# One kernel of four fused layers: the output projection in fp32r parts, another order in the opening, another form of the last multiply

## The reference

```
x = x + L0(x)  # conv over 16 tokens (taps from cond) -> Wp -> B_t = softplus, C_t = tanh; u = x@Ws
               # state = decay*state + dt*B_t*u_t ;  y = C_t*state (64 wide) ; y @ Wo + bo
x = x + L1(x)  # LSTM: a = x@Wx + b + h@Wh ; i,f,o = sigmoid, g = tanh ; c = f*c + i*g ; h = o*tanh(c)
x = x + L2(x)  # token shift, 16 experts by hashed token id: relu(x@wk)**2 @ wv, times a sigmoid gate
x = x + L3(x)  # threshold t per (sequence, feature): L3(x) = x * (|x| >= t)
```

## Time and profile before

| | us |
|---|---|
| median of three runs | 4284.19 |
| profiled execution, its own time | 4276.5 |
| its span, first to last instruction | 4274.8 |
| TensorE busy, share of the span | 3840.3 (90%) |
| VectorE | 3104.3 (73%) |
| ScalarE | 1775.6 (42%) |
| GpSimd | 618.9 (14%) |

### The profile page before, as it was taken

One profiled execution on the slowest core, in us unless ns is written; L12 is line 12 of the kernel. 1 busy time (PEld: TensorE's weight loads), 2 busy tenths in 40 slices (PEclk: granted clock), 3 DMA queues, 4 the chain that ended last, 5 costly groups with the idle time before them and its releaser, 6 DMA issues. The chain is left out here.

```text
span 4274.8 us, 115998 instructions
## 1 busy us (share of the span) xinstructions
PE 3840.3 (90%) x45058; PEld 2624.1 (61%) x45058; DVE 3104.3 (73%) x9883; ACT 1775.6 (42%) x5459; POOL 618.9 (14%) x657
## 2 busy tenths in 40 slices
PE   3799999999999999999999999999599999989900
PEld 3466666666656666665666666665378878869900
DVE  8777787777777777787777787755454455439989
ACT  2233433333433333433333433333244444338866
POOL 4011110110110110110110111110100000005634
PEclk8899999999999999999999999999899999999955
DMA  5211001111001111010011010000234333415412
GB/s 209 88 31 36 26 29 31 31 32 33 26 29 31 30 31 35 26 33 27 28 32 36 26 33 26 26 19 12 104 118 158 137 118 128 154 59 163 155 71 86
DMA packets 143014, 267.65 MB, mean 63 GB/s; under 512 B 19589, under 2 KB 85637, under 8 KB 139458
## 3 DMA queue, kind: packets, MB, share of 16 engines
q1 hardware_dynamic: 120896, 185.19, 12.9%
q0 software_dynamic: 17696, 66.79, 4.3%
q10 hardware_dynamic: 3938, 8.96, 0.6%
HBM read 177.33 MB, written 83.92 MB: 61 GB/s over the span
## 5 line engine op out<-in xcount | busy, mean ns | idle before, releaser
L424 PE MATMUL bank<-buf,buf 128*16 128x256 f32 x32768 | 1873.3, 380 | 68.5 <-DVE buf L695 56.8
L424 PEld LDWEIGHTS bank<-buf,buf 128*16 128x16 f32 x32768 | 906.3, 97 | 904.7 <-DVE buf L695 101.9
L797 PE MATMUL bank<-buf,buf 128*128 128x256 f32 (+1 forms) x3584 | 1181.7, 330 | 25.2 <-DVE buf L1182 22.4
L798 PE MATMUL bank<-buf,buf 128*128 128x256 f32 (+1 forms) x3584 | 1121.3, 313 | 0.0
L799 PE MATMUL bank<-buf,buf 128*128 128x256 f32 (+1 forms) x3584 | 1120.6, 313 | 0.0
L611 DVE SCALAR_TENSOR_TENSOR buf<-buf,buf,buf 128x256 f32<-128x256 f32 x1920 | 880.4, 485 | 0.8 <-issue 0.8
L673 DVE STREAM_TRANSPOSE buf<-bank 128x256 f32<-128x256 f32 x1024 | 458.7, 448 | 544.5 <-PE bank L424 510.6
L797 PEld LDWEIGHTS bank<-buf,buf 128*128 128x128 f32 x3584 | 677.1, 189 | 275.9 <-issue 237.6
L570 ACT ACTIVATE buf<-buf 128x96 f32<-128x96 f32 x1024 | 290.6, 284 | 1208.4 <-DVE buf L678 1208.0
L799 PEld LDWEIGHTS bank<-buf,buf 128*128 128x128 f32 x3584 | 678.7, 189 | 41.2
L798 PEld LDWEIGHTS bank<-buf,buf 128*128 128x128 f32 x3584 | 679.9, 190 | 38.5
(11 more groups left out here) (132 smaller groups left out, 3035.8 us busy)
## 6 DMA issues: line engine op xcount, KB each, us to landing
buf<-in_wk SPq DMA_DIRECT2D x16, 2048.0 KB, 9.7
buf<-in_wv SPq DMA_DIRECT2D x16, 2048.0 KB, 9.8
buf<-in_xT SPq DMA_DIRECT2D x62, 496.0 KB, 3.9
buf<-x_scratch SPq DMA_DIRECT2D x31, 544.0 KB, 4.3
buf<-in_xT SPq DMA_DIRECT2D x32, 512.0 KB, 3.7
expert_in_scratch<-buf POOLq DMA_DIRECT2D x16, 1024.0 KB, 22.2
x_scratch<-buf SPq DMA_DIRECT2D x32, 512.0 KB, 5.0
buf<-expert_in_scratch SPq DMA_DIRECT2D x16, 1024.0 KB, 11.7
```

The source lines that it names most:

```text
L424: last = mm(gate_ps[hf][32 * j:32 * j + B, 0:HCOLS], hist[:, k, at_step(slot_at)], wh[:, k, j * GCOLS + hf * HCOLS:j * GCOLS + (hf + 1) * ...
L797: nc.tensor.matmul(out, left[0], right[0], start=first, stop=False)
L798: nc.tensor.matmul(out, left[0], right[1], start=False, stop=False)
```

## The change

It does four things.

1. **Output projection by parts.** y and Wo are cut into high and low parts in fp32r. The 64 rows of high y and 64 rows of low y stand above each other (`y_pair`, 128 rows) against high Wo twice (`wo_pair`); a second matmul takes high y again with ones (`y_high`, 97 rows used) against low Wo, high bo and low bo (`wo_rest`). So eight fp32r matmuls of 128 and 97 rows stand where four fp32 matmuls of 65 rows stood. ScalarE makes two copies of y (`state_high`) and VectorE the low part (`split_state`), in step 8 of a tile, as the fifth state part. In the opening Wo is loaded twice and bo twice, ScalarE makes three copies and VectorE two subtractions and two fills.
2. **Low parts of Wx on VectorE.** The four subtractions of 128x2048 go from GpSimd to VectorE (`split_wx`), two ahead of tile 0's state parts, two behind them.
3. **Order of the opening.** Wx is loaded behind the small loads, now fourteen. The convolution of tile 2 (the third) is split: its first half ahead of tile 1's state parts, its second half behind tile 1's additions.
4. **Mask.** VectorE makes a factor, 1 or 2, as `(ax >= level) + 1` from one tensor and one column, and GpSimd multiplies it with x, in place of adding.

```diff
-    wo = carve(D)[0:N_STATE + 1]
+    wo_pair, wo_rest = carve(D, dt=F32R), carve(D, dt=F32R)
...
-    y = carve(LTILE)[0:N_STATE + 1]
+    y = carve(LTILE)[0:N_STATE]
+    y_pair, y_high = carve(LTILE, dt=F32R), carve(LTILE, dt=F32R)
     turned_g = [carve(8, 32) for _ in range(2)]
+    wo = carve(D, at=carve.last - 4 * 8 * 32)
...
+    bo_rows, ones = mix.rearrange("p k n -> p (k n)"), rows[:, 0:LTILE]
+    BO_HIGH, BO_LOW, OUT_ROWS = 64, 96, 97
...
-        (wo[N_STATE:], ins["bo"]), (bp_b, ins["bp"][0]), (bp_c, ins["bp"][1]), (bs, ins["bs"]),
+        (wo[N_STATE:], ins["Wo"]), (bo_rows[BO_HIGH:BO_HIGH + 1], ins["bo"]), (bo_rows[BO_LOW:BO_LOW + 1], ins["bo"]), (bp_b, ins["bp"][0]), (bp_c, ins["bp"][1]), (bs, ins["bs"]),
...
-            for k in range(KD):
-                pool.wait_ge(s["wx_hi_ready"], k + 1)
-                g.tensor_tensor(wx_lo[:, k, :], wx_raw[:, k, :], wx_hi[:, k, :].bitcast(F32), ALU.subtract)\
-                    .then_inc(s["wx_ready"], 1)
...
             def outputs(m, q):
+                pe.wait_ge(s["y_high_ready"], 2 * m + 2)
                 pe.wait_ge(s["y_ready"], m + 1)
                 if later(m, 1):
                     pe.wait_ge(s["x1_ready"], 2 * m - 1 + q)
                 if q == 1 and later(m, 3):
                     pe.wait_ge(s["rows_ready"], 2 * (m - 3) + 1)
                 for k in (2 * q, 2 * q + 1):
-                    last = mm(out_ps[q][:, (k - 2 * q) * LTILE:(k - 2 * q + 1) * LTILE], wo[:, k * P:(k + 1) * P], y,
-                              start=True, stop=True)
+                    part = out_ps[q][:, (k - 2 * q) * LTILE:(k - 2 * q + 1) * LTILE]
+                    mm(part, wo_pair[:, k * P:(k + 1) * P], y_pair, start=True, stop=False)
+                    last = mm(part, wo_rest[0:OUT_ROWS, k * P:(k + 1) * P], y_high[0:OUT_ROWS], start=False, stop=True)
                 last.then_inc(s["out_done"], 1)
...
-                    act.wait_ge(s["y_ready"], m)
+                    act.wait_ge(s["y_made"], m)
...
+            def state_high(m):
+                act.wait_ge(s["y_made"], m + 1)
+                if later(m, 1):
+                    act.wait_ge(s["out_done"], 2 * m)
+                a(y_pair[0:N_STATE], y, ACT.Copy).then_inc(s["y_high_ready"], 1)
+                a(y_high[0:N_STATE], y, ACT.Copy).then_inc(s["y_high_ready"], 1)
...
-            act.dma_start(wx_raw, ins["Wx"]).then_inc(s["wx_landed"], 16)
+            act.wait_ge(s["rest_zeroed"], 1)
             for dst, src in small:
                 act.dma_start(dst, src).then_inc(s["small_landed"], 16)
+            act.dma_start(wx_raw, ins["Wx"]).then_inc(s["wx_landed"], 16)
             act.dma_start(wh, ins["Wh"]).then_inc(s["wh_landed"], 16)

             act.wait_ge(s["small_landed"], small_loads)
+            act.wait_ge(s["rest_zeroed"], 2)
+            a(y_high[N_STATE:], ones[N_STATE:], ACT.Copy).then_inc(s["y_ones"], 1)
+            a(wo_pair, wo, ACT.Copy).then_inc(s["wo_high"], 1)
+            a(wo_rest[N_STATE:], bo_rows[N_STATE:], ACT.Copy).then_inc(s["wo_high"], 1)
...
+                    if ahead >= 2 and st == SCAN_AT + 4:
+                        state_high(n + 2)
...
-                    dve.wait_ge(s["out_done"], 2 * m)
-                v.scalar_tensor_tensor(out=y[0:N_STATE].rearrange("p (t b) -> p t b", b=B),
+                    dve.wait_ge(s["y_high_ready"], 2 * m)
+                v.scalar_tensor_tensor(out=y.rearrange("p (t b) -> p t b", b=B),
                                        in0=state.rearrange("p b t -> p t b"), scalar=delta,
                                        in1=c_gate.rearrange("p (t b) -> p t b", b=B), op0=ALU.mult,
-                                       op1=ALU.mult).then_inc(s["y_ready"], 1)
+                                       op1=ALU.mult).then_inc(s["y_made"], 1)
+
+            def split_state(m):
+                dve.wait_ge(s["y_high_ready"], 2 * m + 1)
+                v.tensor_tensor(y_pair[N_STATE:], y, y_pair[0:N_STATE].bitcast(F32),
+                                ALU.subtract).then_inc(s["y_ready"], 1)

             def state_part(m, i):

-                (add_soft, drive_of, scan, gate_state)[i](m)
+                (add_soft, drive_of, scan, gate_state, split_state)[i](m)
...
+            nc.vector.memset(bo_rows, 0.0).then_inc(s["rest_zeroed"], 1)
+            nc.vector.memset(ones, 1.0).then_inc(s["rest_zeroed"], 1)
...
+            dve.wait_ge(s["wo_high"], 2)
+            v.tensor_tensor(wo_rest[0:N_STATE], wo[0:N_STATE], wo_pair[0:N_STATE].bitcast(F32),
+                            ALU.subtract).then_inc(s["wo_ready"], 1)
+            v.tensor_tensor(wo_rest[BO_LOW:OUT_ROWS], bo_rows[BO_LOW:OUT_ROWS], wo_rest[BO_LOW:OUT_ROWS].bitcast(F32),
+                            ALU.subtract).then_inc(s["wo_ready"], 1)
...
-            for m in range(2):
-                for i in range(4):
-                    state_part(m, i)
-                for q in range(2):
-                    add_block(m, 0, m, q)
-                for q in range(2):
-                    convolve(m + 1, q, 0, CONVS // 2)
+            def split_wx(k):
+                dve.wait_ge(s["wx_hi_ready"], k + 1)
+                v.tensor_tensor(wx_lo[:, k, :], wx_raw[:, k, :], wx_hi[:, k, :].bitcast(F32),
+                                ALU.subtract).then_inc(s["wx_ready"], 1)
+
+            for k in range(2):
+                split_wx(k)
+            for i in range(5):
+                state_part(0, i)
+            for k in range(2, KD):
+                split_wx(k)
+            for q in range(2):
+                add_block(0, 0, 0, q)
+            for q in range(2):
+                convolve(1, q, 0, CONVS // 2)
+            convolve(2, 0, 0, CONVS // 2)
+            for i in range(5):
+                state_part(1, i)
+            for q in range(2):
+                add_block(1, 0, 1, q)
+            convolve(2, 1, 0, CONVS // 2)
...
-                    if ahead >= 2 and SCAN_AT <= st < SCAN_AT + 4:
+                    if ahead >= 2 and SCAN_AT <= st < SCAN_AT + 5:
                         state_part(n + 2, st - SCAN_AT)
...
-                g.tensor_tensor(final[i % 2], masked[i % 2], x3_of(u), ALU.add).then_inc(s["final_ready"], 1)
+                g.tensor_tensor(final[i % 2], factor[i % 2], x3_of(u), ALU.mult).then_inc(s["final_ready"], 1)
...
-                v.scalar_tensor_tensor(out=masked[i % 2], in0=ax[i][:, 0:T], scalar=column(level, i),
-                                       in1=x3_of(u), op0=ALU.is_ge, op1=ALU.mult).then_inc(s["masked_ready"], 1)
+                v.tensor_scalar(factor[i % 2], ax[i][:, 0:T], column(level, i), 1.0, ALU.is_ge,
+                                ALU.add).then_inc(s["factor_ready"], 1)
```

More of the change, by code:

```diff
@@ L159, in recur_phase @@
              "small_landed", "wx_landed", "wh_landed", "zeros_made", "zero_stored", "wx_hi_ready", "wx_ready",
-             "window_zeroed", "bufs_zeroed", "gate_zeroed", "y_ones", "small_ready", "conv_done", "proj_part",
+             "window_zeroed", "bufs_zeroed", "gate_zeroed", "rest_zeroed", "wo_high", "wo_ready", "y_ones", "y_made", "y_high_ready", "small_ready", "conv_done", "proj_part",
              "u_part", "gate_c_ready", "soft_abs", "soft_exp", "soft_ready", "bt_ready", "drive_ready",
@@ L434, in _ @@
             pe.wait_ge(s["y_ones"], 1)
+            pe.wait_ge(s["wo_ready"], 2)
             for q in range(2):
@@ L555, in _ @@
             soft_last(0)
+            state_high(0)
             for q in range(2):
@@ L561, in _ @@
             soft_last(1)
+            state_high(1)
             for q in range(2):
@@ L1221, in mask_phase @@
     flag, side, places, ones = carve(T + 1), carve(T), carve(T + 1), carve(T)
-    masked = [carve(T) for _ in range(2)]
+    factor = [carve(T) for _ in range(2)]
     final = [carve(T) for _ in range(2)]
@@ L1226, in mask_phase @@
     names = ["places_made", "abs_ready", "half_ready", "inv_ready", "pi_ready", "rv_ready", "limit_ready",
-             "cum_ready", "sides_ready", "chosen_ready", "level_ready", "masked_ready", "final_ready"]
+             "cum_ready", "sides_ready", "chosen_ready", "level_ready", "factor_ready", "final_ready"]
     s = {n: ctx.enter_context(nc.semaphore("mk_" + n)) for n in names}
@@ L1279, in unit @@
             def unit(u, i, before):
-                pool.wait_ge(s["masked_ready"], u + 1)
+                pool.wait_ge(s["factor_ready"], u + 1)
                 if later(u, 2):
                     pool.wait_ge(stored[i % 2], 16 * before)
-                g.tensor_tensor(final[i % 2], masked[i % 2], x3_of(u), ALU.add).then_inc(s["final_ready"], 1)
+                g.tensor_tensor(final[i % 2], factor[i % 2], x3_of(u), ALU.mult).then_inc(s["final_ready"], 1)
             units(pool, unit)
@@ L1290, in absolute @@
                 if later(u, DEEP):
-                    act.wait_ge(s["masked_ready"], u - DEEP + 1)
+                    act.wait_ge(s["factor_ready"], u - DEEP + 1)
```

1 line of the change is left out of this document (removed).

## The result

The changed kernel takes 4221.45 us (median of 4 runs, 4220.06 to 4222.89) against 4284.23 us (4283.78 to 4284.87, 4 runs): ratio 0.9853, 95% interval 0.9836 to 0.987. That is 62.8 us less, where 61.5 were forecast. The profiled execution took 4221.9 us with a span of 4220.2. Against the profiled execution of before the gain is 54.6 us only.

The account below looks back on a forecast made before the run. TensorE was taken to bound the recurrence, VectorE the opening and last stage. Gains of 20.5 + 24.0 + 17.0 = 61.5 us off the 4284.2 median gave 4222.7 us; range 4209 to 4243.

Parts of the forecast that it names:

- Opening: Before the recurrence: low parts of Wx, load order and split convolution bring the first transpose to 121.0; gain 20.5 us.
- the last meeting with GpSimd: End of the opening: 1 us of GpSimd added to the last half convolution of 12.8, giving 121.0.
- No convolution instruction over 1.5 us: Opening: a sign expected in the new profile, where two VectorE instructions had taken 9.10 us before.
- Recurrence: Output matmuls in steps 10 and 11: 0.40 us saved per step over thirty tiles, 24.0 us; bounds 12 and 29.
- cover: Step 8 of a tile: VectorE's new low part fits into its idle time before the next transpose, 0.5 us left.
- Rival B: Recurrence: outputs' saving given back by a delayed transpose in step 8 or new GpSimd-VectorE meetings; 37.5 us gain, chance 0.07.
- Last stage: The one-or-two multiplier on VectorE takes 485 instead of 751 ns in 64 units, 17.0 us.
- the upper bound of 21: Last stage: the gain if the register operation of x3's address also leaves VectorE, 21 us.
- The form's term: Last stage: reading one tensor and a column instead of two tensors saves 0.266 us per unit, 17.0 us.
- a column 60 ns: Last stage: a column operand costs VectorE's instruction about 60 ns more, by 751 against 692.

Follow-up runs that it names:

- run 3: Changed kernel with the low parts of Wx on GpSimd again: 4232.9 us, 0.9882 of before.
- run 4: Changed kernel with the third convolution whole and last, as before: 4224.68 us, 0.9863 of before.
- run 9: Changed kernel with Wx issued ahead of the small loads, as before: 4225.1 us, 0.9873 of before.
- run 2: Changed kernel with the output projection of before, small loads still first: 4251.38 us, 0.9924 of before.
- run 1: Changed kernel with the last stage of before (three-operand form, GpSimd adds): 4243.7 us, 0.9906 of before.
- run 8: Changed kernel with the old last stage, but every unit reads the first row of x3, so no address is computed: 4233.42 us, 0.9891 of before.
- run 10: Changed kernel with a constant 0.5 for the column in the last stage's multiplier: 4216.15 us, one execution.
- run 7: Changed kernel with the output projection of before and the opening's four low parts of x1 on VectorE: 4233.89 us, 0.9893 of before.
- run 5: The kernel before, unedited, profiled once more, on the second chip: 4278.63 us.
- run 11: The kernel before with the output projection by parts alone: 4263.4 us, 0.9964 of before.
- run 6: Changed kernel with the opening's four low parts of x1 on VectorE instead of GpSimd: 4213.37 us, 0.9847 of before.
- run 12: Changed kernel with the opening's low parts of x1 on VectorE and one small VectorE instruction less in the last stage: 4212.51 us, 0.9844 of before.

## Why the prediction was right

**Opening, 20.5 forecast, 19.5 measured.** Step by step: convolution from 18.8 (18.85), its end 44.2 (44.0), soft chain to 50.0 (49.68), products from 62.5 (61.92), first half of tile 2 from 88.2 (88.47), second soft chain at 101.0 (100.99). The only miss is at the end: for the last meeting with GpSimd I took 1 us, and the pair of L625 took 2.68 instead of 0.73, 1.95 more; with that the first transpose stands at 121.98 and not 121.0. "No convolution instruction over 1.5 us" holds, just: the longest took 1.48 (at 60.57). Runs 3, 4 and 9 priced the parts at 11.6, 3.6 and 6.2 us; these overlap, so they need not add to 19.5.

A price that I did not see was the danger in this part: 12 us hang on whether GpSimd's second low part of x1 gets its turn ahead of a row of thirty. In the changed kernel and in run 2 it starts at the end of the same pair of L625 (L602 there), 0.11 and 0.12 us ahead of the first of the thirty. In the changed kernel it ran at once (1.31) and the first of the thirty waited (1.48), and so in runs 1, 4, 8, 9 and 10; in run 2 all thirty went first. Run 7 shows the price by taking the meeting away. Nor does a row always keep GpSimd out: in the kernel before, the same low part began 0.03 us behind the first of a row and took 1.56 us, and the second of that row waited (1.49):

```profile
77.30 12.97 DVE L611 SCALAR_TENSOR_TENSOR buf<-buf,buf,buf 128x256 f32<-128x256 f32 x30
77.33 1.56 POOL L294 TENSOR_TENSOR buf<-buf,buf 128x512 fp32r<-128x512 f32 x1 [0.43 <-ACT buf L514]
```

What decides who goes first is not shown. The Trainium skill (SBUF — State Buffer, SBUF: two separate sides) says that the port pair of VectorE and GpSimd is a lock held for a whole instruction, and that the other "fully blocks". By that rule GpSimd could get in between any two of the thirty; it did in the kernel before at 77.33, but not in 13.68 us in run 2, nor in 11.22 in run 3.

**Recurrence, 24.0 forecast.** The term was 0.40 per step; steps 10 and 11 measured 0.38, 22.9 us over 30 tiles, in every kernel with the parts. Step 8 kept its cover (0.41 us left, 0.5 forecast). The first comparison of profiles gave only 12.1, and that was no fault of the step: 4.2 us go with the chip (run 5), for by their patterns the two profiles are of chips that differ. The kernels of the other two chips, whose recurrence is the changed one (runs 8 to 10), took 2882.1 to 2883.7 us, against 2898.76 and 2900.85 for before: 17 us net. So 6 us of 22.9 are given back inside the loop. Rival B's idea, small new meetings and waits, is right in kind and a quarter of its size. About 2 us stand in steps 4, 6 and 8 (mostly 0.2 to 0.3 us in a few tiles each); 3.0 to 3.5 us in steps 15 and 0 of tiles 11, 12, 19 and 20, where the program's loop of eight tiles begins again. Neither seems to belong to the output projection as such: run 11, with nothing but it, pays 0.9 us at these returns and 22.9 are left to it but for 0.1 to 2.2; run 7, without it, pays 2.6 there; run 6 has 1.6 us less in steps 4, 6 and 8 than runs 8 to 10.

**Last stage, 17.0 forecast, 22.5 measured, above the upper bound of 21.** The form's term was right (16.4 by run 8), by the durations forecast: 485 ns (486), a column 60 ns (59 by run 10), GpSimd's multiply as its add. What was mis-sized is the register operation, which I put at nothing in the sum and only into the bound, with 4 us; it costs 6.2 us (run 8), 0.097 per unit. Run 1 shows that the 22.5 are all of this edit.

**Sum.** On the first chip the kernel before was not profiled, so its recurrence is missing from a sum there; the medians give 62.8. On the other chips the profiles give 20 + 17 + 22.5 = 59.5. By times it is 62.2 from run 8 (45.8 and the form's 16.4), 60.2 from run 9 (54.0 and its 6.2) and 59.8 from run 10 (4279.1 - 4216.15 - 3.1). The forecast of 61.5 is the sum of a recurrence 7 us too good and a last stage 5.5 us too poor: two misses that cancel. The mechanism of each part was right; that the sum came within 2 us is luck.

Still open: what makes VectorE start 0.2 us later in step 15 on one chip; why the loop's two returns cost 1 to 3.5 us more, by the kernel, than in the kernel before, for which no run was made; what decides whether GpSimd gets its turn ahead of a row of VectorE; and some 4 us between run 11's median and its profile. The gains of 62.8 on the first chip and 59.8 to 62.2 on the others can't be told apart by a measurement here.

Runs 6 and 12 are the fastest kernels, 65.8 and 66.6 us under before against 62.8 for the changed one. The intervals overlap, and run 12 adds nothing to run 6 that a measurement here can tell. But 62.8 is from another chip: on their own chips the changed kernel would gain 59.8 to 62.2 by the sums above, so they are some 4 to 7 us ahead of it. Their profiles show it in two places: the first transpose at 118.4 and 118.5 us (121.1 to 122.2 in runs 8 and 10), and the recurrence at 2877.9 us (2882.1 to 2883.7 in runs 8 to 10). Why low parts that moved in the opening shorten the loop, no run shows.

## What to carry to other kernels

Where an instruction leaves an engine that bounds a loop, count the address arithmetic that leaves with it, and look whether the instruction stood in a wait: one that did is worth nothing (run 12). Ask of each GpSimd instruction which VectorE row it will meet, for a long row without a gap can, but need not, hold it up for the whole row, and TensorE behind it. Before a gap between two profiles is explained, check by a profile of the old kernel on the new chip that it is not the chip.

## What the runs showed of the hardware

- A GpSimd subtraction of 128x512 took 1.31 us, and 13.68 beside thirty two-tensor instructions of VectorE that went on at 0.40 us each (run 2). In the kernel before one that began 0.03 us behind the first of such a row took 1.56, and the second of the row waited. When GpSimd's long ones (4.54 us) held the turn, each VectorE instruction waited for one (run 3).
- A column operand cost VectorE's instruction 59 ns (486 against 427, run 10); an address from a register cost 97 ns per unit of the last stage (run 8 against run 1).
- A wait of VectorE on its own instruction took 0.20 us behind a scan's end; an instruction of 128x1 (0.13 us) placed in it cost nothing.
- TensorE's granted clock stood at 0.53 in the 5 us in which the products began after a rest, for the most part at the lower of its levels (1.2 of 2.4 GHz). With products that began 1.3 us earlier (run 6), full clock came 4.9 us earlier.
- The same program of the recurrence took 4.2 us more on one of three chips, each used once, always at the same three steps of a tile, with TensorE's matmuls at the same distances.
